# One transformer layer with a routed feed-forward on one core: where the patch embedding of the coming block stands in a six-stage software pipeline

## Chip, cores and metric

The kernel runs on one core of one Trainium2 chip, in one launch, all in float32. The metric is the device time of that launch in microseconds, the median of several runs.

## What is computed

32 images are cut into 36 patches of 768 numbers, embedded into 256 dimensions, and given a class token and position rows: 32 x 37 = 1184 tokens. One attention and one mixture-of-experts feed-forward follow, both on normalised input and both added to it:

```python
h = tok(x, W, b, pos_embd)                        # (32, 37, 256), class token in front
h = h + attn(layernorm(h))                        # q, k = rope(silu(x Wq)), rope(silu(x Wk)); 16 heads of 16
                                                  # out = (tril(q k^T)) v, no softmax
                                                  # out * sigmoid(x Wg1 Wg2), layernorm, @ Wo
h = h + moe(layernorm(h))                         # 32 experts of 4 groups, top 2 groups, top 6 experts;
                                                  # one shared expert; 1 of 16 anchor experts by the top expert
```

## The kernel before

**Tiles and blocks.** A tile (`TILES`) is three images, 111 tokens; there are eleven, the last with two images. Two tiles make a block (`BLOCKS`); there are six, block 5 holding the last tile alone, 74 tokens.

**Two halves of the program.** In the front half the blocks go through embedding, attention and routing. For each block the DVE (VectorE) works out, in `choose` and `place`, which row of a DRAM table `rows_d` each token takes in each of its seven lists (six experts and an anchor), and GpSimd writes the token's normalised row there by an indirect DMA (`scatter`, L385, one instruction L389 for a tile and choice, 77 in all). In the second half 112 list tiles of 128 rows are taken from `rows_d`, put through their expert's two matmuls, and added into `sums_d` by one indirect DMA each, again on GpSimd (`add_rows`, L404, instruction L409). At the end four copies of the sums are read back and added to `h` (L1217, L415).

**What orders the work.** Every engine has its own instruction list, written out by hand, and semaphores between them. The front half is a software pipeline: `stage(j)` (L289) names for j = -1 to 6 the block `coming` = j+1 (embedded in this stage), `ahead` = j (projected to q, k, v and gate), `mid` = j-1 (energies and attention, output projection) and `last` = j-2 (routed and ranked). The loops over j stand at L622 for TensorE (PE), L818 for ScalarE (ACT) and L1104 for the DVE. "Stage j" below means this j, and "mask of stage j" the DVE's first instruction of `mask_energy` in it.

**One stage on PE** (L622 to L668), for j = 2 to 4: `embed(coming, 0)`; `energies` of mid's first tile; `stay_busy(2)` (two matmuls whose result nobody reads, into B3, L517); `second_transposes(last)`; `stay_busy(1)`; `energies` of the second tile, in which each strip waits for the DVE to have masked the same strip of the first tile (L508); `attend` tile one, `route(last)`, `attend` tile two; `normed_transposes(ahead)`; `out_project(mid)`; `embed(coming, 1)`; `rank(last)`; `project(ahead)` (q and k, then v); `rotate`, `gate_inner`, `gate`. `embed` multiplies six chunks of the patches by the weights into bank B0, and its `pe.wait_ge(h_emb, b)` waits until the DVE has taken the block before out of B0. Every float32 matmul is two passes in the records, so an embedding of one tile is "x12".

**The first stages are different.** Stage -1 embeds block 0 and sends nine `stay_busy` matmuls behind it. Block 1's first tile is embedded at the end of stage 0 and its second in stage 1, between the energies. Stage 1 also folds the second layer norm's weights into the output projection: ACT scales `w_o` (`widen`, L732), PE multiplies (`fold`, L436), ACT copies a bias (`fold_bias`, L742), the DVE finishes (`fold`, L1084), and `embed` of block 2 waits for that (L427).

**One stage on the DVE** (L1104 to L1134), for j = 2 to 5: `mask_energy` of both tiles (L1036); `apply_gate(mid)` (L1046), which waits for both `attend`; `choose(last)`; `attended(mid)` (L1053 to L1068); `place(last)`, whose last instruction `slot` (L990) lets GpSimd go on with the block; `embedded(coming)` (L995: adds the position rows into `h`, L998, and takes the moments); `rope(ahead)` (L1019 to L1029), in which `add_bias` (L1007) stands; `norms()` (L916), one pass of inverse square roots for `last`'s coming second norm and for `coming`'s first. In stage 1 `embedded(1)` and its `norms` stand between the two masks, with the DVE's `fold` behind them.

**ACT** (L818 to L837) does `second_norm`, `second_copy`, `first_norm`, `scores`, `normed_copy`, `squares`, `qkv_copies`, `split_heads` (after the DVE's rope, releases the energies), `gate_tanh`.

**SyncE** issues the loads in one queue (L298 to L340): half of block 0's chunks, small constants, `w_qkv` and other constants (semaphore `consts`), patches of block 1, the weights of `rest`, patches of blocks 2 to 5, then the filling of `rows_d` and the experts' weights.

Of the kernel before, what the change touches and what calls it, by code (L numbers as in the profile page):

```python
# [78 lines left out]
def build(nc, pt, wt, posr, brow, wqkv, wo, wg1, wg2, lnwb, gwt, gbias, sgu, sd, wx,  # L79
          ident_c, cmask_c, turn_c, parity_c, cs_c, before_c, small_c, out):  # L80
    with ExitStack() as ctx:
# [216 lines left out]
        def _(sp):  # L298
# [6 lines left out]
            sp.dma_start(w_qkv[:, :, :], wqkv).then_inc(ld["consts"], 16)  # L305
            sp.dma_start(w_g1[:, :, :], wg1).then_inc(ld["consts"], 16)
            for dst, src in ((turn, turn_c), (w_g2, wg2), (parity, parity_c)):
                sp.dma_start(dst[:, :], src).then_inc(ld["consts"], 16)
            sp.dma_start(cossin[:, :, :], cs_c).then_inc(ld["consts"], 16)
# [5 lines left out]
            load_patches(1)  # L315
            for dst, src in ((w_o, wo), (ln_wb, lnwb), (w_route, gwt), (w_sgu, sgu)):
                sp.dma_start(dst[:, :, :], src).then_inc(ld["rest"], 16)
# [101 lines left out]
        def _(pe):  # L419
            def embed(b, i):  # L420
                t, at = BLOCKS[b][i], i * TT
                if b:
                    pe.wait_ge(ld[f"patch{b}"], 16)
                if i == 0 and b:
# [3 lines left out]
                for c in range(PC):  # L428
# [4 lines left out]
                if i == len(BLOCKS[b]) - 1:  # L433
                    m.then_inc(emb_ps, 1)
# [24 lines left out]
            def project(b):  # L459
                n = SIZES[b]  # L460
                pe.wait_ge(xnT_ok, b + 1)
                for half in range(2):
# [5 lines left out]
                    m.then_inc(qk_ps, 1)  # L468
                for t in BLOCKS[b]:
# [152 lines left out]
            for j in range(-1, NB + 1):  # L622
                coming, ahead, mid, last = stage(j)
                tiles = BLOCKS[mid] if mid is not None else []
                if coming is not None and j not in (0, 1):
                    embed(coming, 0)
                if j == -1:
                    embed(coming, 1)
                    stay_busy(9)
                if j == 0:  # L630
                    pe.wait_ge(ld["consts"], 16 * 8)
                if mid is not None:
                    energies(mid, tiles[0])
                if j == 1:
                    embed(ahead, 1)
                if last is not None and coming is not None:
                    stay_busy(2)
                if last is not None:
                    second_transposes(last)
                if last is not None and coming is not None:  # L640
                    stay_busy(1)
                for t in tiles[1:]:
                    energies(mid, t)
                if j == 1:
                    fold()
                if mid is not None:
                    attend(mid, tiles[0])
                if last is not None:
# [3 lines left out]
                if ahead is not None:  # L652
                    normed_transposes(ahead)
                if j == 1:
                    embed(coming, 0)
# [647 lines left out]
```

## Time and profile before

| | us |
|---|---|
| runs before: median (lowest, highest) of 3 | 471.47 (469.03, 471.80) |
| the profiled execution: its own time | 472.09 |
| its span, first to last instruction | 470.2 |
| GpSimd busy in it | 291.5 |
| PE busy, DVE busy, ACT busy | 369.0, 260.5, 202.1 |

The profile is one execution. Busy times of different engines overlap; a busy PE is not a PE at its peak. "Granted clock" is the share of full speed that TensorE's clock had (1.00 is 2.4 GHz, 0.50 is 1.2 GHz). The end of a matmul is modelled, so where the clock changes, what waits for it is the better witness.

### The profile page before, as it was taken

Reading aid. Unit: us, or ns where it says so; the run is one execution under the profiler, and the core shown is the slowest. Engines: PE = TensorE matmul, PEld = TensorE weight load, DVE = VectorE, ACT = ScalarE, POOL = GpSimd, SP = SyncE. Lnnn points to the kernel's source line nnn. Section 1 sums busy time; section 2 is a strip of 40 time slices with the busy share of each in tenths; the row PEclk is TensorE's granted clock in tenths of the full one; section 3 lists DMA queues with packets and bytes.
Section 4 is the critical chain, followed back from the end, with each engine's and each line's share of the span. In section 5 each row is a group of like instructions: output and inputs, shape, how many; then the busy total and the mean of one; then the engine's idle time right before and its main releaser. Section 6 shows DMA issues by size and latency. Waiting matters only on the chain.

```text
span 470.2 us, 10193 instructions
## 1 busy us (share of the span) xinstructions
PE 369.0 (78%) x2492; PEld 303.7 (65%) x2493; DVE 260.5 (55%) x1088; ACT 202.1 (43%) x581; POOL 291.5 (62%) x205
## 2 busy tenths in 40 slices
PE   6897999889987977367788799998999889998000
PEld 4666868568675865246566577887878787886000
DVE  0346668969588686674355445444454444444135
ACT  1132152341525222201266567677676767676000
POOL 3000000685848838886688888888888888888432
PEclk9998999979979565589599999999999999999655
DMA  8999998232329723893589998999989999997795
GB/s 237 314 338 316 428 366 316 49 84 54 81 67 360 164 56 79 265 321 101 135 149 154 158 157 150 158 160 151 156 146 163 153 151 160 158 153 102 159 265 166
DMA packets 67599, 85.81 MB, mean 182 GB/s; under 512 B 16984, under 2 KB 61446, under 8 KB 67318
## 3 DMA queue, kind: packets, MB, share of 16 engines
q1 hardware_dynamic: 37030, 59.82, 41.1%
q0 software_dynamic: 29680, 24.95, 36.0%
q10 hardware_dynamic: 864, 0.73, 0.5%
q8 instruction: 12, 0.20, 0.2%
q14 instruction: 13, 0.11, 0.1%
HBM read 45.86 MB, written 39.47 MB: 181 GB/s over the span
## 4 chain that ended last, share of the span: by engine, by line
PE 25%; DMA 19%; issue 16%; DVE 13%; POOL 13%; ACT 8%; ACTq 3%; SPq 1%; POOLq 0%; DVEq 0%
DMA sums_d<-e_sb,tok 13%; POOL rows_d L389 7%; PE B L431 6%; POOL sums_d L409 5%; PE B L466 3%; ACT UPW L852 3%; ACTq L276 2%; PE B L700 2%; DMA W<-sums_d 2%; PE B L529 2%; DMA e_sb<-rows_d 2%; ACT e_sb L875 2%; PE B L509 2%; DVE e_sb L1036 2%; PE B L712 2%
## 5 line engine op out<-in xcount | busy, mean ns | idle before, releaser
L409 POOL DMA_INDIRECT sums_d<-e_sb,tok x112 | 174.1, 1555 | 36.3 <-issue 24.6
L389 POOL DMA_INDIRECT rows_d<-xrow,slot x77 | 105.9, 1375 | 120.3 <-issue 103.9
L700 PEld LDWEIGHTS B<-e_sb,UPW 128*128 128x128 f32 x796 | 107.0, 195 | 10.3 <-issue 3.9
L700 PE MATMUL B<-e_sb,UPW 128*128 128x128 f32 x796 | 110.3, 280 | 0.0
L712 PE MATMUL B<-W,e_sb 128*128 x224 | 75.1, 417 | 21.4 <-issue 11.2
L1208 DVE TENSOR_TENSOR e_sb<-e_sb,B 128x128 f32<-128x128 f32 (+1 forms) x112 | 32.3, 288 | 83.9 <-ACT e_sb L863 58.9
L852 ACT COPY UPW<-W 128x512 f32 (+1 forms) x112 | 63.0, 562 | 0.7 <-issue 0.6
L712 PEld LDWEIGHTS B<-W,e_sb 128*128 128x128 f32 x224 | 34.2, 192 | 36.4 <-issue 35.4
L875 ACT ACTIVATE e_sb<-B,wcol 128x256 f32<-128x256 f32 x112 | 53.1, 474 | 0.0
L1192 DVE COPY e_sb<-B 128x256 f32<-128x256 f32 x112 | 46.9, 419 | 5.3 <-PE B L688 3.7
L688 PE MATMUL B<-ident,e_sb 128*128 128x128 f32 x224 | 44.7, 283 | 6.1 <-DMA e_sb<-rows_d 5.7
L874 ACT COPY tok<-tok_of 128x1 int32 (+1 forms) x112 | 21.5, 192 | 60.4 <-DMA sums_d<-e_sb,tok 36.1
L431 PE MATMUL B<-W 128*111 128x256 f32 (+1 forms) x132 | 35.8, 425 | 4.6 <-DMA W<-in_pt 4.6
L863 ACT ACTIVATE e_sb<-B 128x128 f32<-128x128 f32 (+1 forms) x112 | 30.8, 275 | 16.4 <-PE B L700 9.3
L688 PEld LDWEIGHTS B<-ident,e_sb 128*128 128x128 f32 x224 | 28.1, 145 | 8.3 <-DMA e_sb<-rows_d 4.5
L431 PEld LDWEIGHTS B<-W 128*111 128x111 f32 (+1 forms) x132 | 24.8, 196 | 12.7 <-DMA W<-in_pt 5.2
L1194 DVE TENSOR_TENSOR wcol<-e_sb,fresh (+1 forms) x112 | 17.8, 159 | 23.0 <-issue 18.1
L1036 DVE TENSOR_TENSOR e_sb<-B,causal 111x444 f32<-111x444 f32 (+1 forms) x44 | 23.6, 597 | 11.9 <-PE B L509 11.9
L767 ACT ACTIVATE W<-B 128x444 f32<-128x444 f32 (+1 forms) x12 | 6.0, 501 | 47.8 <-PE B L466 47.8
L1217 DVE TENSOR_TENSOR h<-h,W 112x256 f32<-112x256 f32 (+3 forms) x15 | 12.7, 867 | 19.3 <-DMA W<-sums_d 11.3
L466 PE MATMUL B<-W 128*128 128x222 f32 (+1 forms) x96 | 22.1, 396 | 0.6 <-ACT W L761 0.6
L466 PEld LDWEIGHTS B<-W 128*128 128x128 f32 x96 | 20.2, 234 | 1.3 <-ACT W L761 0.8
(167 smaller groups left out, 457.4 us busy)
## 6 DMA issues: line engine op xcount, KB each, us to landing
e_sb<-rows_d SPq DMA_DIRECT2D x112, 152.5 KB
rows_d<-padrow SPq DMA_DIRECT2D x1, 7320.0 KB, 34.5
W<-in_wx SPq DMA_DIRECT2D x1, 7027.0 KB, 50.6
sums_d<-padrow SPq DMA_DIRECT2D x4, 1408.0 KB, 22.5
W<-in_wx SPq DMA_DIRECT2D x1, 4576.0 KB
W<-in_wx SPq DMA_DIRECT2D x9, 478.5 KB
W<-in_pt SPq DMA_DIRECT2D x4, 666.0 KB, 8.7
sums_d<-e_sb,tok POOLq DMA_INDIRECT x112
```

The costliest lines, as they stand in the source:

```text
L389: pool.indirect_dma_start(rows_d, bass.IndirectOffsetOnAxis(ap=slot[0:n, t, j:j + 1], axis=0), xrow[0:n, t, :], None).then_inc(done, 16)
L409: pool.indirect_dma_start(sums_d[c], bass.IndirectOffsetOnAxis(ap=tok[:, c:c + 1], axis=0), Y[:, c, :], None, compute_op=ALU.add).then_inc ...
L431: m = pe.matmul(B[0][0:TILES[t], i * D:(i + 1) * D], patch_view(b)[:, c, at:at + TILES[t]], w_patch[:, c, :], start=c == 0, stop=c == PC - 1)
L466: m = pe.matmul(B[4 + half][:, c * BT:c * BT + n], w_qkv[:, k, lo:lo + P], xnT[:, k, 0:n], start=k == 0, stop=k == KC - 1)
L688: m = pe.transpose(B[u % 2][:, k * P:(k + 1) * P], G[:, u % 4, k * P:(k + 1) * P], ident[:, :])
L700: mm = pe.matmul(B[2 + u % 2][:, m * P:(m + 1) * P], UPW[:, u % 2, at:at + P], GT[:, u % 2, k, :], start=k == 0, stop=k == KC - 1)
L712: pe.matmul(B[6 + u % 2][:, 0:D], H[:, u % 2, :], W[:, bass.ds(e, size)][:, at:at + D], start=True, stop=True).then_inc(D_ps, 1)
L852: act.copy(UPW[:, u % 2, 0:n], weights[:, 0:n]).then_inc(upw_ok, 1)
L875: act.activation(Y[:, u % 4, :], B[6 + u % 2][:, 0:D], ACT.Copy, scale=wcol[:, bass.ds(i, 1)]).then_inc(Y_ok, 1)
L1036: dve.tensor_tensor(energy[0:n, i, 4 * r:4 * r + 4, 0:n], B[4 + r][0:n, 0:4 * n].rearrange("p (h t) -> p h t", h=4), causal[0:n, 0:n].unsq ...
L1192: dve.tensor_copy(GT[:, v % 2, :, :].rearrange("p k s -> p (k s)"), B[v % 2][:, 0:D]).then_inc(gt_ok, 1)
L1208: dve.tensor_tensor(H[0:n, u % 2, :], S[0:n, u % 2, :], ups, ALU.mult).then_inc(H_ok, 1)
```

## The change

- SyncE: the patches of block 1 are loaded ahead of `w_qkv` instead of behind `cossin`.
- Stage -1 on PE: three `stay_busy` matmuls instead of nine, and behind them the whole embedding of block 1. The DVE takes it out (`embedded(1)`, `norms`) in stage 0 ahead of `rope(0)`.
- The fold (`widen`, both `fold`, `fold_bias`) moves from stage 1 to the end of stage 0.
- `embed` gets a range of chunks. In stages 2 and 3 the second tile of the coming block is embedded in two halves of three chunks, one between the two energies and one behind the second; in stage 1 that place takes block 2's first tile, and its second stays behind the output projection. The three `stay_busy` matmuls of stages 2 to 4 go.
- `normed_transposes(ahead)` stands between the two `attend` in stage 1; elsewhere it stays behind both.
- `project` is split: q and k (`project_heads`) come right behind the output projection, then `rank(last)`, then v (`project_values`).
- DVE: `embedded(coming)` moves from behind `place` to between the masks and `apply_gate` (stages 2 to 4; in stage 1 it stays ahead of `rope`). `add_bias` moves out of `rope` to behind `norms`. `norms` waits for `xn_ok` of the block ahead.

The diff, cut to its lines and those next to them, indentation shortened:

```diff
@@ -302,17 +302,17 @@
...
         sp.dma_start(dst[:, :], src).then_inc(ld["consts"], 16)
+
+    def load_patches(b):
+        lo = PC * FIRST[b]
+        sp.dma_start(patches[:, lo:lo + PC * SIZES[b]], pt[:, lo:lo + PC * SIZES[b]]).then_inc(ld[f"patch{b}"], 16)
+
+    load_patches(1)
     sp.dma_start(w_qkv[:, :, :], wqkv).then_inc(ld["consts"], 16)
...
     sp.dma_start(cossin[:, :, :], cs_c).then_inc(ld["consts"], 16)
-
-    def load_patches(b):
-        lo = PC * FIRST[b]
-        sp.dma_start(patches[:, lo:lo + PC * SIZES[b]], pt[:, lo:lo + PC * SIZES[b]]).then_inc(ld[f"patch{b}"], 16)
-
-    load_patches(1)
     for dst, src in ((w_o, wo), (ln_wb, lnwb), (w_route, gwt), (w_sgu, sgu)):
@@ -417,20 +417,20 @@
...
 def _(pe):
-    def embed(b, i):
+    def embed(b, i, lo=0, hi=PC):
         t, at = BLOCKS[b][i], i * TT
-        if b:
+        if b and lo == 0:
             pe.wait_ge(ld[f"patch{b}"], 16)
-        if i == 0 and b:
+        if i == 0 and b and lo == 0:
             pe.wait_ge(h_emb, b)
...
                 pe.wait_ge(fold_ok, 1)
-        for c in range(PC):
+        for c in range(lo, hi):
             if b == 0 and i == 0:
...
                           w_patch[:, c, :], start=c == 0, stop=c == PC - 1)
-        if i == len(BLOCKS[b]) - 1:
+        if i == len(BLOCKS[b]) - 1 and hi == PC:
             m.then_inc(emb_ps, 1)
@@ -456,7 +456,7 @@
...

-    def project(b):
+    def project_heads(b):
         n = SIZES[b]
@@ -466,6 +466,8 @@
...
             m.then_inc(qk_ps, 1)
+
+    def project_values(b):
         for t in BLOCKS[b]:
@@ -622,50 +624,52 @@
...
         tiles = BLOCKS[mid] if mid is not None else []
-        if coming is not None and j not in (0, 1):
-            embed(coming, 0)
+        two = coming is not None and len(BLOCKS[coming]) > 1
         if j == -1:
-            embed(coming, 1)
-            stay_busy(9)
+            embed(0, 0)
+            embed(0, 1)
+            stay_busy(3)
+            embed(1, 0)
+            embed(1, 1)
         if j == 0:
             pe.wait_ge(ld["consts"], 16 * 8)
+        if coming is not None and j > 1:
+            embed(coming, 0)
         if mid is not None:
             energies(mid, tiles[0])
-        if j == 1:
-            embed(ahead, 1)
-        if last is not None and coming is not None:
-            stay_busy(2)
+        if two and j >= 1:
+            embed(coming, min(j - 1, 1), 0, PC // 2)
+        for t in tiles[1:]:
+            energies(mid, t)
+        if two and j >= 1:
+            embed(coming, min(j - 1, 1), PC // 2, PC)
         if last is not None:
             second_transposes(last)
-        if last is not None and coming is not None:
-            stay_busy(1)
-        for t in tiles[1:]:
-            energies(mid, t)
-        if j == 1:
-            fold()
         if mid is not None:
             attend(mid, tiles[0])
+        if j == 1:
+            normed_transposes(ahead)
         if last is not None:
...
             attend(mid, t)
-        if ahead is not None:
+        if ahead is not None and j != 1:
             normed_transposes(ahead)
-        if j == 1:
-            embed(coming, 0)
         if mid is not None:
             out_project(mid)
-        if coming is not None and len(BLOCKS[coming]) > 1 and j > 0:
+        if j == 1:
             embed(coming, 1)
+        if ahead is not None:
+            project_heads(ahead)
         if last is not None:
...
         if ahead is not None:
-            project(ahead)
+            project_values(ahead)
             rotate(ahead)
...
         if j == 0:
-            embed(coming, 0)
+            fold()
     second_transposes(NB - 1)
@@ -817,9 +821,6 @@
...
         _, ahead, mid, last = stage(j)
-        if j == 1:
-            widen()
-            fold_bias()
         if last is not None:
@@ -833,8 +834,12 @@
...
             qkv_copies(ahead)
+            if j == 0:
+                widen()
             split_heads(ahead)
             gate_tanh(ahead)
+        if j == 0:
+            fold_bias()
     second_norm(NB - 1)
@@ -913,8 +918,10 @@
...

-    def norms():
-
+    def norms(ahead):
+
+        if ahead is not None:
+            dve.wait_ge(xn_ok, BLOCKS[ahead][-1] + 1)
         step(dve.scalar_tensor_tensor(nwt[:, 0, 1:3, :], mv[:, 1:3, :, 1], EPS,
@@ -1017,8 +1024,6 @@
...
         step(dve.tensor_tensor(r, q, cossin[:, 0, :].unsqueeze(1).unsqueeze(1).to_broadcast(shape), ALU.mult))
-        if b:
-            add_bias(b)
         for half in range(2):
@@ -1103,17 +1108,17 @@
...
         coming, ahead, mid, last = stage(j)
+        if j <= 0:
+            embedded(coming)
+            norms(ahead)
         if j == 1:
             dve.wait_ge(ld["rest"], 16 * 8)
-            mask_energy(mid, BLOCKS[mid][0])
-            embedded(ahead)
-            norms()
-            mask_energy(mid, BLOCKS[mid][1])
-            fold()
+        for t in BLOCKS[mid] if mid is not None else []:
+            mask_energy(mid, t)
+        if j == 1:
             add_bias(mid)
-        else:
-            for t in BLOCKS[mid] if mid is not None else []:
-                mask_energy(mid, t)
+        if coming is not None and j > 1:
+            embedded(coming)
         if mid is not None:
@@ -1122,16 +1127,19 @@
...
             place(last)
-        if ahead == 0:
+        if j == 1:
+            embedded(coming)
+        if j == 0:
             dve.wait_ge(ld["consts"], 16 * 8)
             step(dve.tensor_scalar(base[:, :], base0, 1.0, None, ALU.add))
+        if ahead is not None:
             rope(ahead)
-        if coming is not None and j != 0:
-            embedded(coming)
-        if ahead is not None and ahead > 0:
-            rope(ahead)
-        if j != 0:
-            norms()
+        if j == 0:
+            fold()
+        if j > 0:
+            norms(ahead)
+        if ahead is not None and j > 0:
+            add_bias(ahead)
     choose(NB - 1)
...
```

## Rows read from the trace of the kernel before

**Rows 1.** Groups of GpSimd instructions: count, busy us, mean ns, idle us before them

```profile
L409 POOL DMA_INDIRECT sums_d<-e_sb,tok x112 | 174.1, 1555 | 36.3 <-issue 24.6 <-ACT e_sb L875 11.7
L389 POOL DMA_INDIRECT rows_d<-xrow,slot x77 | 105.9, 1375 | 120.3 <-issue 103.9 <-DVE slot L990 16.4
```

**Rows 2.** GpSimd's timeline: start us, duration us, instruction, idle time and its releaser

```profile
84.29 1.55 POOL L389 DMA_INDIRECT rows_d<-xrow,slot  x1 [79.58 <-issue]
...
111.62 1.35 POOL L389 DMA_INDIRECT rows_d<-xrow,slot  x1 [4.18 <-DVE slot L990]
...
141.24 1.35 POOL L389 DMA_INDIRECT rows_d<-xrow,slot  x1 [5.84 <-DVE slot L990]
...
170.81 1.48 POOL L389 DMA_INDIRECT rows_d<-xrow,slot  x1 [6.38 <-DVE slot L990]
...
212.57 1.36 POOL L389 DMA_INDIRECT rows_d<-xrow,slot  x1 [0.30 <-issue]
...
231.24 1.62 POOL L409 DMA_INDIRECT sums_d<-e_sb,tok  x1 [0.35 <-issue]
```

**Rows 3.** The DVE's timeline in stages 1 to 6, columns as in rows 2

```profile
32.71 2.20 DVE L1036 TENSOR_TENSOR e_sb<-B,causal 111x444 f32<-111x444 f32 x4 [4.36 <-PE B L509]
...
43.46 0.62 DVE L1046 SCALAR_TENSOR_TENSOR W<-W,B 128x444 f32<-128x444 f32 x1 [0.51 <-PE B L529]
...
64.81 2.20 DVE L1036 TENSOR_TENSOR e_sb<-B,causal 111x444 f32<-111x444 f32 x4 [1.90 <-PE B L509]
67.74 2.20 DVE L1036 TENSOR_TENSOR e_sb<-B,causal 111x444 f32<-111x444 f32 x4 [0.73 <-PE B L509]
71.04 0.62 DVE L1046 SCALAR_TENSOR_TENSOR W<-W,B 128x444 f32<-128x444 f32 x1 [1.10 <-PE B L529]
...
83.20 0.69 DVE L998 TENSOR_TENSOR h<-B,W 111x512 f32<-111x512 f32 x1
...
85.00 1.08 DVE L1019 TENSOR_TENSOR W<-W,cossin 128x888 f32<-128x888 f32 x1
...
91.45 2.19 DVE L1036 TENSOR_TENSOR e_sb<-B,causal 111x444 f32<-111x444 f32 x4
...
121.80 2.20 DVE L1036 TENSOR_TENSOR e_sb<-B,causal 111x444 f32<-111x444 f32 x4 [1.86 <-PE B L509]
...
148.93 2.20 DVE L1036 TENSOR_TENSOR e_sb<-B,causal 111x444 f32<-111x444 f32 x4
...
157.97 0.62 DVE L1046 SCALAR_TENSOR_TENSOR W<-W,B 128x444 f32<-128x444 f32 x1 [3.46 <-PE B L529]
...
175.25 1.57 DVE L1036 TENSOR_TENSOR e_sb<-B,causal 74x296 f32<-74x296 f32 x4
```

**Rows 4.** PE's timeline

```profile
13.21 4.05 PE L517 MATMUL B<-W 128*128 128x256 f32 x18
...
18.88 0.57 PE L456 MATMUL B<-ident,W 111*128 111x111 f32 x4 [1.63 <-ACT W L749]
...
47.26 1.03 PE L543 MATMUL B<-W 128*111 128x257 f32 x4
...
49.71 2.83 PE L431 MATMUL B<-W 128*111 128x256 f32 x12
...
90.36 1.02 PE L509 MATMUL B<-W 32*111 32x222 f32 x16 [0.91 <-ACT W L786]
...
104.77 3.75 PE L431 MATMUL B<-W 128*111 128x256 f32 x12
```

**Rows 5.** Two windows: length, busy PE, PEld, DVE, ACT, POOL, granted clock, DMA share, GB/s

```profile
99.90:106.70 6.80, 6.80 (x21) 5.37 (x22) 5.97 (x43) 1.77 (x2) 5.58 (x5) 0.50 0.39 94
...
151.00:171.20 20.20, 19.90 (x139) 16.52 (x134) 14.00 (x70) 5.28 (x12) 11.38 (x10) 0.50 0.59 152
```

**Rows 6.** The DMA issue at 8.42 us: count, size, us to landing

```profile
W<-in_pt SPq DMA_DIRECT2D x1, 666.0 KB, 8.1
```

**Rows 7.** ACT's timeline

```profile
29.93 0.90 ACT L737 ACTIVATE W<-W,ln_wb 128x256 f32<-128x256 f32 x2
```

## Prediction

> **What bounds the kernel now.** I begin with the groups of GpSimd's instructions [rows 1]. There are two: 77 scatters of 1.375 us and 112 additions of 1.555 us. Each is followed by some 0.30 us in which the queue waits for nothing shown, so a scatter costs 1.65 us and an addition 1.86 us. GpSimd's timeline [rows 2] then gives the frame. It starts at 84.29 us and from there it never has more than a few microseconds of rest. The reader is to see the three gaps, 4.18, 5.84 and 6.38 us, each ended by the DVE's `slot`: GpSimd has written a block's 14 tile-choices (14 x 1.65 = 23.2 us) and waits for the next block's places. From 170.81 on there is no such wait up to 231.24, where the additions begin 0.35 us behind the last scatter; 112 x 1.86 = 208 us later they are done, and some 31 us of reading back, adding and storing close the span of 470.2 us. So the end is the start of the fourth block's scatters plus 299.4 us, as long as nothing else in the front half is later than GpSimd. It nearly is: SyncE takes list rows only when the last anchor scatter (issued 212.57) has landed, and the shared expert on PE and DVE ends at about that time. A gain thus needs both: places for block 3 earlier, and the front half's computing earlier by as much.
>
> The DVE's timeline [rows 3] gives the stages. First masks of stages 1 to 6 stand at 32.71, 64.81, 91.45, 121.80, 148.93 and 175.25: stages of 32.1, 26.6, 30.4, 27.1 and 26.3 us, against GpSimd's 23.2. Which engine makes them so long is read from the idle time ahead of the rows. In stage 2 the DVE idles before both masks (1.90 and 0.73) and before the gate (1.10), and from 71.04 to 91.45 it works without a break: 20.4 us. PE's timeline [rows 4] has the other case, the first energies of stage 3 at 90.36, waiting 0.91 for ACT and so for the DVE's rope. So a stage is a piece M to A (mask to gate) in which PE and DVE wait for each other, and a piece A to M in which the DVE alone decides, unless PE is late with its embeddings. It was late in stage 3: the output projection and the embedding ran at half clock (3.75 against 2.83 us [rows 4]; granted clock 0.50 from 99.9 to 106.7 [rows 5]), PE reached the energies late and the DVE idled 1.86 before 121.80 [rows 3].
>
> **The front, stages -1 to 1.** Six of 18 passes of `stay_busy` remain: 4.05/3 = 1.35, PE free at 14.56 [rows 4]. Block 1's patches are issued some 2.8 us earlier, at 5.59; with the 8.1 us of [rows 6] they land at 13.7. Left where they were they would land at 16.5. The constants now behind them were all issued before 8.42 and, at that same delay, are there by 16.5 to 17; PE wants them at 20. Cost nothing. Two embeddings at 2.83 [rows 4], slightly overlapping, end at 20.2. The first transposes stood at 18.88, so all of stage 0 slips by 1.3. `widen` (two of its four activations 0.90 [rows 7], so at most 1.8) now stands ahead of `split_heads` on ACT, and the fold on PE (8 passes at 2.83/12, 1.9) ahead of the energies; behind the fold wait the energies alone, and the DVE's fold runs while PE does them. Ahead of those energies stood an embedding of 2.8. Energies and mask: + 1.3 - 2.8 + 1.9 + 0 to 1.2 of waiting for `widen`; I take +0.7 for the last, since about half of it lies under the gate matmuls. M1 is 32.71 + 1.1 = 33.8.
>
> M to A in stage 1 was 43.46 - 32.71 = 10.75; a whole embedding, a normalisation and the fold lay in it. New: the first mask and the wait for the second energies, 67.74 - 64.81 = 2.93 as in stage 2; then 3.30 (71.04 - 67.74), plus PE's second half embedding of 1.4 pushed ahead of the attention, less the 0.4 or so by which attention then waits less for the mask. The transposes between the attends replace a routing. So 7.2, A1 = 41.0 instead of 43.46. Output projection (49.71 - 47.26 = 2.45) after 0.7 for the gate: the second embedding starts at 44.15 instead of 49.71. From there to M2 PE's order is the same work, except that the embedding goes before q and k in both; PE had 15.1 us to 64.81. M2 = 59.25, **5.6 us earlier**. The DVE, freed of nothing in this stretch, ends attended, embedded, rope, norms and bias at about 58, so PE decides.
>
> **Stages 2 to 4, M to A.** Stages 2 and 3: 6.23 of before (71.04 - 64.81), plus half an embedding 1.4, plus the second transposes, now behind the second energies, 0.57 (as four matmuls in [rows 4]), less 0.2 to 0.4 of mask waiting. I take 8.0. The first half embedding lies in the wait for the mask. Bounds for the two halves together: 0, if all is cover, and 2 x 1.9 at half clock (half of 3.75); taken 1.4. The DVE fills this wait with `embedded`, 85.00 - 83.20 = 1.80 [rows 3]. Stage 4 has one tile coming and no halves: 6.6. The dropped `stay_busy` lay in the same waits and gives nothing back.
>
> **A to M.** The DVE's 20.41 less 1.80 is 18.6; `add_bias` only changes its place. PE's 2.8 of embedding is out of it, q and k start right behind the output projection, and the embedding that stays ahead of the energies is done about 1 us before rope: no stage is PE's any more. The wait put into `norms` costs nothing: `xn_ok` comes from ACT before PE's transposes, 15 us earlier. `rank` behind q and k costs nothing at full clock: `place` ends 12.2 us after A (83.20 - 71.04) and takes them some 1.3 before that, and PE has them by 0.7 + 2.45 + 3.8 + 1.9 = 8.9 at most (16 and 8 passes at 2.83/12).
>
> So M3 = 59.25 + 8.0 + 18.6 = 85.85, A3 93.85, M4 = 112.45, A4 = 119.05, M5 = 137.65. Stage 5 as before, 157.97 - 148.93 = 9.04 to A5 = 146.7, 17.28 more to M6, with 0.7 for ranks behind q and k at half clock (0.50 from 151.0 to 171.2 [rows 5]): 164.7. Against before: 5.6, 5.6, 9.35, 11.3, 10.6 us earlier.
>
> **GpSimd.** First start was A2 + 13.25, the fourth A5 + 12.84 [rows 2, 3]. New: 67.25 + 13.25 = 80.5; 93.85 + 12.84 = 106.7; 131.9; 146.7 + 12.84 + 0.7 = 160.2, each later than 23.2 us behind the one before, so gaps of 3.0, 2.0 and 5.1 remain. The fourth is 10.6 earlier than 170.81, computing is earlier by the same, and the additions run in the same rhythm: span 470.2 - 10.6 = 459.6. The profiled execution took 472.09, 1.9 beyond its span, and stands 0.6 above the median of the runs, 471.47. So 461.5 in its own terms, 460.9 in the median's; **I say 461.**
>
> **A rule against the change.** The dropped matmuls kept TensorE occupied. In the rows the clock is 0.50 for 6.8 us behind a light stretch in stage 3 and for 20.2 us in stage 5, where no embedding stands among the small matmuls [rows 5]. The Trainium skill, "TensorE: Matmul & The Clock Gate", in its Part 1 on the clock gate, says that the throttled state is the default and activity lifts it; in its section on a second failure mode it has small pauses between groups of matmuls enough to make the clock oscillate. By that rule the stages without dummies would run at half clock and the kernel would take the time of the slow rival below; by the rows, real embeddings of full width now stand where the dummies stood, except in stage 4.
>
> **Rivals.**
> 1. *Only the front gains.* PE's lateness in stage 3 was the clock's, and some other wait (ACT's table and copies between transposes and scores, late rank) holds stages 3 and 4 at 30.4 and 27.1 us. For: the DVE, which I call the bound, is merely close to it. Against: it works 20.4 us unbroken in stage 2. Then everything is 5.6 earlier: 465.9.
> 2. *Clock lost in stages 2 to 4; slower.* If the clock falls between masks and gate, half embeddings and attention double: M to A grows from 8.0 by the 2.8 that stage 5 shows over stage 2 (9.04 - 6.23) and by 1.4 more for the second half, and the ranks, now behind q and k, come 2 us late for `place`: 6.2 us a stage. Three stages are 18.6 - 10.6 = 8 us slower: 479. It decides from the second such stage on.
> 3. *GpSimd alone.* Stages come down to 23.2, no gaps: fourth start 80.5 + 69.6 = 150.1, 20.7 earlier: 451. Against: the DVE has 18.6 + 4.4 of masks + 1.8 + waits, over 25.
> 4. *It doesn't do what it says*: block 1's patches are late, and stage 0 slips by more than stage 1 wins. Price 16.5 - 14.56 = 2: 463.
>
> **Chances and range.** Forecast 0.55 (457 to 464.5); rival 1 0.20; rival 2 0.09 (with one stage cold, 467; with two, 473); rival 3 0.06; rival 4 0.10. The range 454 to 469 takes in rivals 1 and 4, one cold stage, and below, stage 5 at full clock (2.4 us less from M to A, no rank delay) with the half embeddings wholly covered (up to 2 x 1.4); it leaves out the rest of 2 and part of 3. About 1%, 4.7 us, is what a measurement can tell from no change. Faster by more (under 466.8): 0.79. Within: 0.14. Slower: 0.07.
>
> **What would show it.** First energies-mask of stages 2 to 6 near 59, 86, 112, 138, 165; GpSimd's first and fourth block at 80.5 and 160, three gaps of 2 to 5 us; PE idle about 1 us before the energies of stages 3 and 4; M to A near 8, no DVE wait from A to M. Wrong if: masks of stage 4 or 5 less than 7 us earlier (rival 1), granted clock 0.50 before the gates of stages 2 to 4 (rival 2), the additions starting later than right behind the last scatter (the front's computing is then the bound).

## Result and the profile after

The changed kernel takes 465.8 us (median of 20 runs) against 470.04 (20 runs) of the kernel before: ratio 0.9907, 95% interval 0.9883 to 0.9931. A second group of runs gave 466.64 against 468.95, ratio 0.9956 (0.9930 to 0.9981). So the change gains 2 to 4 us, and the forecast of 461 (10.5 gained) was too good by some 5. The profiled execution has a span of 463.5 and took 465.33; that of before took 472.09, 2 us above its own kernel's median of 20, so 6.7 us between the two traces stand for 4.2 between the medians.

The page of the changed kernel: granted clock and GpSimd in 40 slices (tenths), and GpSimd's two groups with count, busy us, mean ns and idle time before them.

```profile
span 463.5 us, 10136 instructions
...
POOL 3000000886858668886788888888888888888433
PEclk9999999999596555588599999999999999999555
...
L409 POOL DMA_INDIRECT sums_d<-e_sb,tok x112 | 174.1, 1555 | 35.2 <-issue 26.8
L389 POOL DMA_INDIRECT rows_d<-xrow,slot x77 | 107.3, 1394 | 113.2 <-issue 101.0
```

The groups are those of [rows 1]: 1.56 and 1.39 us, the same rhythm, so the gain is in when the work starts. The clock's digits are near full speed up to slice 10, then 5 in slice 11 (115.9 to 127.5 us), 9 in slice 12, and 5 or 6 in slices 13 to 17. Next GpSimd's timeline, to be laid beside [rows 2].

```profile
80.87 1.55 POOL L389 DMA_INDIRECT rows_d<-xrow,slot  x1 [76.15 <-issue]
...
107.06 2.04 POOL L389 DMA_INDIRECT rows_d<-xrow,slot  x1 [2.78 <-DVE slot L997]
...
135.65 2.04 POOL L389 DMA_INDIRECT rows_d<-xrow,slot  x1 [4.36 <-DVE slot L997]
...
164.89 1.35 POOL L389 DMA_INDIRECT rows_d<-xrow,slot  x1 [4.99 <-DVE slot L997]
...
206.33 1.36 POOL L389 DMA_INDIRECT rows_d<-xrow,slot  x1 [0.30 <-issue]
...
213.93 1.35 POOL L389 DMA_INDIRECT rows_d<-xrow,slot  x1 [2.94 <-issue]
...
225.53 1.62 POOL L409 DMA_INDIRECT sums_d<-e_sb,tok  x1 [0.30 <-issue]
```

First start 80.87 (before 84.29), fourth 164.89 (170.81), additions from 225.53 (231.24). The three gaps are 2.78, 4.36 and 4.99; the forecast had 3.0, 2.0 and 5.1, so the second is the one that it missed. The last anchor scatter is issued at 206.33 (before 212.57, the fifth row of [rows 2]). Two scatters behind it GpSimd pauses for 2.94 us with nothing shown that it waits for; the kernel before has such a pause too, 2.37 us ahead of 219.61. The fourth start is 5.92 earlier, the first addition 5.71, and 1.0 more is won in the additions and their end. The DVE's masks and gates, to be laid beside [rows 3]:

```profile
59.66 2.20 DVE L1041 TENSOR_TENSOR e_sb<-B,causal 111x444 f32<-111x444 f32 x4 [1.29 <-PE B L511]
...
67.61 0.62 DVE L1051 SCALAR_TENSOR_TENSOR W<-W,B 128x444 f32<-128x444 f32 x1 [1.15 <-issue]
...
86.05 2.19 DVE L1041 TENSOR_TENSOR e_sb<-B,causal 111x444 f32<-111x444 f32 x4
...
94.58 0.62 DVE L1051 SCALAR_TENSOR_TENSOR W<-W,B 128x444 f32<-128x444 f32 x1 [1.73 <-issue]
...
113.07 2.19 DVE L1041 TENSOR_TENSOR e_sb<-B,causal 111x444 f32<-111x444 f32 x4
116.45 2.20 DVE L1041 TENSOR_TENSOR e_sb<-B,causal 111x444 f32<-111x444 f32 x4 [1.18 <-PE B L511]
...
123.10 0.62 DVE L1051 SCALAR_TENSOR_TENSOR W<-W,B 128x444 f32<-128x444 f32 x1 [3.45 <-PE B L531]
...
141.66 2.19 DVE L1041 TENSOR_TENSOR e_sb<-B,causal 111x444 f32<-111x444 f32 x4
...
151.63 0.62 DVE L1051 SCALAR_TENSOR_TENSOR W<-W,B 128x444 f32<-128x444 f32 x1 [4.40 <-PE B L531]
...
169.69 1.57 DVE L1041 TENSOR_TENSOR e_sb<-B,causal 74x296 f32<-74x296 f32 x4
```

| | before | forecast | measured |
|---|---|---|---|
| first mask, stage 2 | 64.81 | 59.25 | 59.66 |
| first mask, stage 3 | 91.45 | 85.85 | 86.05 |
| first mask, stage 4 | 121.80 | 112.45 | 113.07 |
| mask to gate, stages 2, 3 | 6.23, 7.71 | 8.0, 8.0 | 7.95, 8.53 |
| mask to gate, stage 4 | 7.02 | 6.6 | **10.03** |
| first mask, stage 5 | 148.93 | 137.65 | 141.66 |
| mask to gate, stage 5 | 9.04 | 9.04 | 9.97 |
| first mask, stage 6 | 175.25 | 164.7 | 169.69 |
| fourth block's scatters | 170.81 | 160.2 | 164.89 |

Up to the mask of stage 4 every step is within 0.7 us. Of the 4.7 us missing at the fourth block, 3.4 arise in one place, between mask and gate of stage 4, where the DVE idles 3.45 us for PE. Another 0.6 us was there at the mask of stage 4, and 0.9 comes from mask to gate of stage 5. The windows of the same kernel (length, busy PE, PEld, DVE, ACT, POOL, granted clock, DMA share, GB/s) and PE's timeline of stage 4 say why.

```profile
86.00:113.00 27.00, 24.26 (x201) 18.29 (x199) 22.61 (x94) 10.28 (x22) 20.26 (x15) 1.00 0.31 73
...
114.40:127.60 13.20, 13.20 (x106) 10.41 (x106) 8.08 (x38) 5.37 (x9) 10.76 (x9) 0.50 0.73 260
...
141.70:199.60 57.90, 43.39 (x261) 35.55 (x262) 39.98 (x207) 14.00 (x31) 43.31 (x32) 0.50 0.48 140
```

```profile
107.68 2.82 PE L431 MATMUL B<-W 128*74 128x256 f32 x12
111.49 1.02 PE L511 MATMUL B<-W 32*111 32x222 f32 x16 [0.98 <-ACT W L790]
113.83 3.30 PE L511 MATMUL B<-W 32*111 32x222 f32 x16 [1.32 <-DVE e_sb L1041]
...
117.99 1.71 PE L531 MATMUL B<-e_sb,W 111*32 111x111 f32 x32
...
128.28 3.25 PE L466 MATMUL B<-W 128*128 128x222 f32 x16
```

PE embeds block 5's only tile, waits 0.98 for ACT, does the first energies, waits 1.32 for the mask, and in the second energies the clock goes to 0.50: 3.30 us for them where the first took 1.02, 1.71 for an attention that takes 0.97 at full clock (91.10 in stage 3 of this trace). It stays there for all of the 13.2 us of the second window with PE busy all the time, is back at 127.8 us in the output projection's second tile, so that q and k (128.28) run at full clock, and is lost again in stage 5 for 57.9 us.

### The profile page after: what moved, and what is told of

It reads as the page before. It is cut to its first block, busy times and chain, and to the rows that moved or that the text cites. A ratio compares the mean times of both kernels' runs of the same rounds, so it can differ in the third digit from the quotient of the medians.

```text
span 463.5 us, 10136 instructions
## 1 busy us (share of the span) xinstructions
PE 366.1 (79%) x2462; PEld 301.3 (65%) x2463; DVE 260.3 (56%) x1088; ACT 201.3 (43%) x581; POOL 293.7 (63%) x205
## 4 chain that ended last, share of the span: by engine, by line
issue 20%; PE 19%; DMA 19%; DVE 14%; POOL 12%; ACT 8%; ACTq 5%; SPq 2%; DVEq 0%; POOLq 0%
DMA sums_d<-e_sb,tok 12%; POOL rows_d L389 7%; PE B L431 4%; POOL sums_d L409 4%; ACT UPW L857 4%; PE B L511 3%; ACTq L276 3%; PE B L531 2%; PE B L466 2%; DMA W<-in_pt 2%; DMA W<-sums_d 2%; ACT e_sb L880 2%; DVE h L1225 2%; DMA rows_d<-xrow,slot 1%; PE B L545 1%
## 5 line engine op out<-in xcount | busy, mean ns | idle before, releaser
L409 POOL DMA_INDIRECT sums_d<-e_sb,tok x112 | 174.1, 1555 | 35.2 <-issue 26.8
L389 POOL DMA_INDIRECT rows_d<-xrow,slot x77 | 107.3, 1394 | 113.2 <-issue 101.0
L704 PEld LDWEIGHTS B<-e_sb,UPW 128*128 128x128 f32 x796 | 107.0, 195 | 10.5 <-issue 4.9
L431 PE MATMUL B<-W 128*111 128x256 f32 (+1 forms) x132 | 33.7, 404 | 6.1 <-DMA W<-in_pt 5.9
L868 ACT ACTIVATE e_sb<-B 128x128 f32<-128x128 f32 (+1 forms) x112 | 30.8, 275 | 17.7 <-PE B L704 10.4
L431 PEld LDWEIGHTS B<-W 128*111 128x111 f32 (+1 forms) x132 | 22.8, 181 | 14.7 <-DMA W<-in_pt 6.8
L511 PE MATMUL B<-W 32*111 32x222 f32 (+1 forms) x176 | 19.6, 424 | 6.7 <-ACT W L790 4.0
L511 PEld LDWEIGHTS B<-W 32*111 32x111 f32 (+1 forms) x176 | 12.8, 194 | 12.5 <-ACT W L790 5.2
L466 PE MATMUL B<-W 128*128 128x222 f32 (+1 forms) x96 | 19.8, 366 | 0.6 <-ACT W L765 0.6
```

Of the source, the lines that this page charges most:

```text
L389: pool.indirect_dma_start(rows_d, bass.IndirectOffsetOnAxis(ap=slot[0:n, t, j:j + 1], axis=0), xrow[0:n, t, :], None).then_inc(done, 16)
L409: pool.indirect_dma_start(sums_d[c], bass.IndirectOffsetOnAxis(ap=tok[:, c:c + 1], axis=0), Y[:, c, :], None, compute_op=ALU.add).then_inc ...
L431: m = pe.matmul(B[0][0:TILES[t], i * D:(i + 1) * D], patch_view(b)[:, c, at:at + TILES[t]], w_patch[:, c, :], start=c == 0, stop=c == PC - 1)
L511: m = pe.matmul(B[4 + r][0:n, 2 * k * n:2 * (k + 1) * n], qk[strip, KC + k, at:at + n], q_two[strip, :, k, at:at + n], start=True, stop=True)
L704: mm = pe.matmul(B[2 + u % 2][:, m * P:(m + 1) * P], UPW[:, u % 2, at:at + P], GT[:, u % 2, k, :], start=k == 0, stop=k == KC - 1)
L868: act.activation(S[0:n, u % 2, :], B[2 + u % 2][0:n, 0:P], ACT.Silu).then_inc(silu_ok, 1)
```

## The experiments

**The changed kernel again.**

> The changed kernel itself, for a second trace and as the yardstick of this group. Clock theory: the granted clock falls to 0.50 between the two energies of stage 4 again, mask to gate takes about 10.0 us there against the 6.6 forecast, and the time is 4 to 5 us below the kernel before. Rival (the first trace was one chance execution): stage 4 at full clock, mask to gate near 6.6, and more than 6 us gained.

Measured: 466.64, ratio 0.9956 (0.9930 to 0.9981). In its trace stage 4 has half clock from 114 to 124, 10.03 from mask (112.75) to gate (122.78); stage 5's mask at 141.56. The time is 2.3 us under that of before, where 4 to 5 were expected. The loss in stage 4 came in both traces, so it was no chance of the first one.

**The kernel before again.**

> The kernel before, for a second trace. Chance theory (the half-clock stretch from 99.9 to 106.7 us in stage 3 of the first trace is a matter of the execution, not of the order of the work): no such stretch or one elsewhere, stage 3 near 26.6 us instead of 30.4, and a time near 469 instead of 472.1. Rival (the order of stage 3 causes it): half clock in stage 3 again and a stage of 30 us.

```profile
94.00:122.60 28.60, 26.14 (x209) 20.16 (x209) 22.81 (x94) 10.93 (x23) 20.46 (x15) 0.94 0.30 70
...
104.00:107.00 3.00, 3.00 (x11) 2.40 (x10) 2.69 (x19) 0.17 (x1) 2.39 (x3) 0.50 0.36 90
```

Measured: 470.35 us in one run. Stage 3 took 28.65 us (93.99 to 122.64), between the two expectations: half clock again at the same place of the stage, but for 3.4 us (103.8 to 107.2) and not for 6.8 as in [rows 5]. So the length of the stretch is the execution's, and 1.7 of the 30.4 us of stage 3 in the trace that I forecast from were bad luck. There was good luck as well: the first mask of stage 2 stands at 67.34 here, 2.5 later than in [rows 3], behind half clock from 18.4 to 25.2 us, which the first trace does not have.

**Stage 4 filled.**

```diff
+                if j == 4:
+                    stay_busy(3)
                 for t in tiles[1:]:
                     energies(mid, t)
```

> The changed kernel with three matmuls of no use put back between the two energies of stage 4, where no half embedding stands. Clock theory: granted clock 1.00 there, mask to gate 6.6 to 7.1 instead of 10.0, mask of stage 5 near 138.3 instead of 141.7, fourth block's scatters 3 us earlier, and the time 3 us below the changed kernel's. Rival (the DVE's new order or the late ranks hold the stage): mask to gate stays near 10 and the time is the same or up to 1 us longer.

PE, then the DVE, then two windows of this kernel:

```profile
112.86 1.02 PE L511 MATMUL B<-W 32*111 32x222 f32 x16 [1.53 <-ACT W L792]
113.81 1.56 PE L519 MATMUL B<-W 128*128 128x256 f32 x6
115.30 2.38 PE L511 MATMUL B<-W 32*111 32x222 f32 x16
```

```profile
114.44 2.19 DVE L1043 TENSOR_TENSOR e_sb<-B,causal 111x444 f32<-111x444 f32 x4
117.36 2.20 DVE L1043 TENSOR_TENSOR e_sb<-B,causal 111x444 f32<-111x444 f32 x4 [0.73 <-PE B L511]
...
121.05 0.62 DVE L1053 SCALAR_TENSOR_TENSOR W<-W,B 128x444 f32<-128x444 f32 x1 [0.49 <-PE B L531]
```

```profile
114.40:121.00 6.60, 6.60 (x98) 4.80 (x97) 5.36 (x12) 3.37 (x6) 5.38 (x5) 1.00 0.37 83
121.00:137.00 16.00, 12.36 (x70) 10.22 (x69) 14.44 (x69) 5.09 (x14) 12.65 (x10) 1.00 0.93 336
```

Measured: 463.33, ratio 0.9883 (0.9847 to 0.9918), 3.3 below the changed kernel of the same group. Mask to gate is 6.61, the forecast's 6.6, at clock 1.00: 1.4 us of matmuls that nobody reads, laid into a wait, give back 3.4. In its trace the stages stand 1.4 us later (114.44 against 113.07 at this mask) behind half clock from 31.6 to 35.0 us, so the mask of stage 5 stands at 139.86, not at 138.3.

**Stages 4 and 5 filled**, twice. The operands are those of `w_qkv`, since `w_patch` is being overwritten by then.

```diff
+            def fill(n):
+                for _ in range(n):
+                    pe.matmul(B[3][:, 0:D], w_qkv[:, 0, 0:P], w_qkv[:, 0, 0:D], start=True, stop=True)
...
+                if j == 5:
+                    pe.wait_ge(h2_ok, BLOCKS[mid][0])
+                    fill(4)
                 if mid is not None:
                     energies(mid, tiles[0])
                 if two and j >= 1:
                     embed(coming, min(j - 1, 1), 0, PC // 2)
+                if j in (4, 5):
+                    fill(3)
                 for t in tiles[1:]:
                     energies(mid, t)
```

> The changed kernel with unused matmuls in stage 4 (three between the energies, as before) and in stage 5 (four ahead of the energies, three between them). Clock theory: full clock until the gate of stage 5, mask to gate there 6.6 instead of 10.0, the mask of stage 6 3 us earlier than with stage 4 filled alone, GpSimd's gap before block 3 gone, and the time 2 to 3 us below it. Rival (stage 5's small matmuls lose the clock whatever stands among them): mask to gate stays 9 to 10, same time as with stage 4 alone.

> The kernel with stages 4 and 5 filled, again, as the yardstick of this group: ratio to before between 0.978 and 0.986, the time near 461.

```profile
112.81 2.19 DVE L1051 TENSOR_TENSOR e_sb<-B,causal 111x444 f32<-111x444 f32 x4
...
120.33 0.62 DVE L1061 SCALAR_TENSOR_TENSOR W<-W,B 128x444 f32<-128x444 f32 x1 [1.40 <-PE B L536]
...
138.78 2.19 DVE L1051 TENSOR_TENSOR e_sb<-B,causal 111x444 f32<-111x444 f32 x4
...
145.52 0.62 DVE L1061 SCALAR_TENSOR_TENSOR W<-W,B 128x444 f32<-128x444 f32 x1 [1.61 <-PE B L536]
...
161.87 1.57 DVE L1051 TENSOR_TENSOR e_sb<-B,causal 74x296 f32<-74x296 f32 x4
```

```profile
158.38 1.35 POOL L389 DMA_INDIRECT rows_d<-xrow,slot  x1 [1.45 <-DVE slot L1007]
...
219.11 1.62 POOL L409 DMA_INDIRECT sums_d<-e_sb,tok  x1 [0.30 <-issue]
223.91 1.59 POOL L409 DMA_INDIRECT sums_d<-e_sb,tok  x1 [3.18 <-ACT e_sb L890]
```

Measured: 461.61, ratio 0.9809 (0.9766 to 0.9852), and 459.51, ratio 0.9785 (0.9748 to 0.9821). Stage 4's 7.52 from mask to gate is 6.61 in the second trace. From mask to gate stage 5 takes 6.74 (second trace 6.55) instead of 9.97, and the mask of stage 6 comes at 161.87 instead of 169.69. GpSimd's gap before block 3 is 1.45, not gone. The fourth block is 6.5 us earlier than in the changed kernel, the span 4.5: the second list tile's addition waits 3.18 us for its rows, so the first list tiles, and no longer the scatters alone, set the end there. Which of the seven unused matmuls of stage 5 are needed was not tried. This is the time that I had forecast for the change alone.

**More filling.** Against the kernel with stages 4 and 5 filled (the operands now from `w_sgu`):

```diff
-                if j == 5:
+                if j in (5, 6):
                     pe.wait_ge(h2_ok, BLOCKS[mid][0])
-                    fill(4)
+                    fill(4 if j == 5 else 10)
...
-                if j in (4, 5):
+                if j in (4, 5, 6):
                     fill(3)
...
             pe.wait_ge(hs_ok, NB)
+            fill(6, 4)
```

> As fill45, with unused matmuls in stage 6 too (ten ahead of its energies, three behind them) and six ahead of the first list tile. Clock theory: full clock in stage 6's attention and routing, about 1.5 us less from its mask to its choice, and 1 to 3 us less at the first list tiles, where GpSimd waited 3.18 us for the second tile; time 1 to 3 us below fill45. Rival (behind stage 5 the DVE and the scatters alone decide): the same time within 1 us.

Measured: 458.53, ratio 0.9792 (0.9754 to 0.9830). The clock was 1.00 from 140 to 169 us, but the median is only 1.0 us under that of stages 4 and 5 filled in the same group (459.51), its ratio is not below theirs (0.9785), and the intervals cover each other: the two are not told apart.

**Front alone.** Stage -1, the fold and `norms` as changed, from stage 2 on the order as before, except that `add_bias` stays behind `norms`; in stage 1 the embedding stays around the output projection. PE's order against the kernel before:

```diff
                 if j == -1:
-                    embed(coming, 1)
-                    stay_busy(9)
+                    embed(0, 0)
+                    embed(0, 1)
+                    stay_busy(3)
+                    embed(1, 0)
+                    embed(1, 1)
...
-                if j == 1:
-                    embed(ahead, 1)
...
-                if j == 1:
-                    fold()
...
                 if j == 0:
-                    embed(coming, 0)
+                    fold()
```

> The kernel before with the front part of the change alone: block 1 embedded in stage -1, patches and fold earlier; stages 2 to 6 in the old order, with their unused matmuls. My theory (front gains 5.2 by the mask of stage 2, reordered stages then win 3.5 in stage 3 and lose it again in stages 4 and 5): mask of stage 2 at 59.7, time 4 to 6 us below before, the same as the changed kernel within 1.5 us. Rival (the reordered stages carry the gain): time within 2 us of before.

Measured: 466.86, ratio 0.9966 (0.9939 to 0.9994); as fast as the whole change in the same group. The mask of stage 2 came at 63.16, not at 59.7: a half-clock stretch at 37 to 44 us in stage 1, where no half embedding stands between the energies. Stages 2 to 5 then took 26.5, 26.9, 26.3 and 25.5 us (the changed kernel 26.4, 27.0, 28.6 and 28.0), and the fourth block started at 164.81. So in the two traces the new order is 3.5 us ahead at stage 2 and loses that in stages 4 and 5; on balance it gives nothing measurable. Stages 2 and 3 are as long in the old order as in the new: stage 3 has no half-clock stretch here, and its 30.4 us of before are gone without any reordering of it.

**Before, without its nine unused matmuls.**

```diff
-                if last is not None and coming is not None:
-                    stay_busy(2)
                 if last is not None:
                     second_transposes(last)
-                if last is not None and coming is not None:
-                    stay_busy(1)
```

> The kernel before without its nine unused matmuls in stages 2 to 4 and nothing else changed. Clock theory: the granted clock falls between mask and gate of at least one of the three stages, mask to gate there 9 to 10 us instead of 6.2 to 7.7, and the time is 2 to 6 us longer than before. Rival (they did nothing): same time within 1 us.

The gate of stage 4 in the kernel before, 7.02 us behind its mask at 121.80:

```profile
128.82 0.62 DVE L1046 SCALAR_TENSOR_TENSOR W<-W,B 128x444 f32<-128x444 f32 x1 [1.88 <-PE B L529]
```

Measured: 470.77, ratio 1.0036 (1.0013 to 1.0060), 1.8 us longer than before in the same group, a little less than the 2 to 6 expected. In the trace mask to gate of stage 4 is 9.04 us (119.79 to 128.83) instead of 7.02, at a mean clock of 0.55. Stages 2 and 3 take 6.23 and 7.27 from mask to gate, no longer than before, so the loss shows in stage 4 alone. They had been doing something.

**Ranks ahead of q and k.**

```diff
-                if ahead is not None:
-                    project_heads(ahead)
                 if last is not None:
                     rank(last)
                 if ahead is not None:
+                    project_heads(ahead)
                     project_values(ahead)
```

> The changed kernel with the ranks ahead of q and k again. My forecast's term (ranks behind q and k cost nothing at full clock and 0.7 us at half clock in stage 5; q and k earlier gain nothing, since the DVE sets the pace): the same time within 1 us, and no wait of the DVE before the ranks' reading in stage 5. Rival (ranks first hold q and k back until the choice is made): the DVE waits at rope and the stages grow by 1 us or more.

PE behind the output projection of stage 2:

```profile
70.17 0.46 PE L548 MATMUL B<-ones,W 128*111 128x1 f32 x4
72.43 0.62 PE L581 MATMUL B<-chosen,before 111*111 111x48 f32 x4 [1.81 <-DVE chosen L971]
...
74.09 5.99 PE L466 MATMUL B<-W 128*128 128x222 f32 x16
```

Measured: 471.63, ratio 1.0011 (0.9981 to 1.0041): against 0.9907 and 0.9956 of the changed kernel this one place costs 2.6 to 4.9 us, about the whole gain. PE waits 1.81 for the choice, the ranks and then q and k run at half clock, 5.99 us instead of 3.25, PE comes late to the next energies, and stages 2 and 3 take 30.0 and 30.8 us.

**The same with that wait filled** by four unused matmuls into bank B0 (`fill` as above).

```diff
+                if last is not None and coming is not None:
+                    pe.wait_ge(h_emb, coming + 1)
+                    fill(4)
                 if last is not None:
                     rank(last)
```

> The ranks ahead of q and k, as in the run before, but with four unused matmuls (into a free bank) in the wait between output projection and ranks of stages 2 to 4. Clock theory (PE's 1.6 to 1.8 us of waiting for the choice loses the clock, and q and k then take 5.9 us instead of 3.1): q and k near 3.2 us, stages 2 and 3 back at 26.5 to 27.5 us instead of 30.0 and 30.8, time 4 to 6 us below ranks first unfilled. Rival (waiting for the choice itself is what costs): stages stay near 30 and the time near 471.

```profile
71.08 0.46 PE L553 MATMUL B<-ones,W 128*111 128x1 f32 x4
71.40 1.97 PE L524 MATMUL B<-W 128*128 128x256 f32 x8
73.35 0.59 PE L586 MATMUL B<-chosen,before 111*111 111x48 f32 x4
...
74.41 3.23 PE L466 MATMUL B<-W 128*128 128x222 f32 x16
```

Measured: 465.93, ratio 0.9940 (0.9911 to 0.9969), 0.7% or 3.3 us less by the two ratios, where 4 to 6 were expected. The ranks come no earlier: 1.81 us behind the end of the output projection (73.35 behind 71.54, unfilled 72.43 behind 70.63) and 13.10 us behind the mask of stage 2 in both traces. q and k take 3.23 us instead of 5.99, and the stages are 26.7 and 26.8 us. So it is not the wait that costs: the clock lost in it costs 3.3 (30.0 - 26.7) to 4.0 us a stage in these traces. They lie further apart than the kernels do (473.18 and 462.27, the latter the fastest of its 12 runs), so the price in the mean is the 3.3 us of the ratios.

**Embedding taken out late on the DVE**, behind `place`.

```diff
                 if j == 1:
                     add_bias(mid)
-                if coming is not None and j > 1:
-                    embedded(coming)
                 if mid is not None:
                     apply_gate(mid)
...
                 if last is not None:
                     place(last)
-                if j == 1:
+                if coming is not None and j > 0:
                     embedded(coming)
```

> The changed kernel with the DVE taking the coming block out of PSUM behind the placing again, as before the change. My forecast's term (between masks and gate the DVE idles anyway, so this work lies there for nothing): the DVE idles 3 us before the gates of stages 2 and 3 instead of 1.2 to 1.7, these stages grow by about 1.8 us each and the time by 3 to 4. Rival (it only moves the idle time): same time within 1 us.

```profile
60.70 2.20 DVE L1041 TENSOR_TENSOR e_sb<-B,causal 111x444 f32<-111x444 f32 x4 [1.29 <-PE B L511]
...
68.59 0.62 DVE L1051 SCALAR_TENSOR_TENSOR W<-W,B 128x444 f32<-128x444 f32 x1 [2.76 <-PE B L531]
```

Measured: 470.80, ratio 1.0008 (0.9986 to 1.0030); 2.4 to 4.7 us longer than the changed kernel by the ratios. The DVE idles 2.76 before the gate of stage 2 and 2.67 in stage 3, and the stages take 28.1 and 28.9 us, 1.7 and 1.9 more; stage 3 has 3.4 us of half clock in this trace (88.4 to 91.8) which the changed kernel does not have, so stage 2's 1.7 is the clean figure.

**The coming tile embedded whole** behind the second energies.

```diff
-                if two and j >= 1:
-                    embed(coming, min(j - 1, 1), 0, PC // 2)
                 for t in tiles[1:]:
                     energies(mid, t)
                 if two and j >= 1:
-                    embed(coming, min(j - 1, 1), PC // 2, PC)
+                    embed(coming, min(j - 1, 1))
```

> The changed kernel with the coming tile embedded whole behind the second energies instead of in two halves around them. My forecast's term (the first half lies in the wait for the mask): mask to gate grows by 1.4 us in stages 2 and 3, from 8.0 to 9.4, and by as much in stage 1, time 3 to 5 us longer than the changed kernel. Clock theory adds: the wait between the energies is then empty, and half clock may begin in stage 2 or 3 already; then 6 us or more. Rival (the halves are cosmetic): same time within 1 us.

```profile
94.17 3.31 PE L511 MATMUL B<-W 32*111 32x222 f32 x16 [1.33 <-DVE e_sb L1039]
97.41 4.72 PE L431 MATMUL B<-W 128*111 128x256 f32 x12
```

Measured: 476.11, ratio 1.0148 (1.0101 to 1.0195), 9 to 11 us longer than the changed kernel by the ratios: mask to gate 10.9 in stage 2 and 11.9 in stage 3. The clock goes at the empty wait between the energies or soon behind it (in stage 3 3.31 us for the second energies and 4.72 for an embedding of 2.8) in stages 1, 2 and 3, from 36.4, 67.1 and 94.4 us, as the clock theory's addition had it.

## Why the prediction was wrong

**What bounds the kernel: right.** GpSimd's rhythm and the start of the fourth block set the end; 5.9 us there became 6.7 in the span. The sum of the miss at the fourth block, 4.7 us: 0.6 up to the mask of stage 4, 3.4 and 0.9 from mask to gate of stages 4 and 5, and 0.3 less behind that. One reading was off: "From 170.81 on there is no such wait up to 231.24" passes over the pause of 2.37 us at 219.61. It is 2.94 us in the changed kernel, 0.6 more.

**The front: right.** Mask of stage 2 forecast 59.25, measured 59.66. It is nearly the whole of what the change gains: with it alone the time is 466.86, with all of the change 466.64. Block 1's patches held PE until 14.90 instead of 14.56, and the embeddings ended at 20.3.

**Mask to gate, the step that failed.** "Stage 4 has one tile coming and no halves: 6.6. The dropped `stay_busy` lay in the same waits and gives nothing back." The first sentence holds at full clock (6.61 with stage 4 filled). The second is the error: I priced the dropped matmuls by the PE time they take, and that is nothing, but what they kept was the clock. In stages 2 and 3 the half embeddings took over that duty, in stage 4 nothing did, and it cost 3.4 us there. The sign that I had set for rival 2, 0.50 ahead of a gate of stages 2 to 4, came in stage 4. The Trainium skill, "TensorE: Matmul & The Clock Gate", Part 1, has half speed as the default that activity lifts. The traces agree in stage 4: 0.50 from 114.4, and 1.00 there with three matmuls more. Stages 2 and 3, with embeddings where the unused matmuls stood, stayed at 1.00 up to there (86.0 to 113.0 in the windows). I had named stage 4 as the exception and then put no microsecond on it; rival 2 with one cold stage stood at 467, at 6.2 us a stage where 3.4 were measured.

**Rival 1's number, not its mechanism.** "Everything is 5.6 earlier: 465.9" is all but the measured 465.8, by luck. No other wait holds stages 3 and 4 at 30.4 and 27.1 us: stage 3 takes 27.0, the masks of stages 4 and 5 are 8.7 and 7.3 us earlier, above its limit of 7, and stage 4 filled takes 25.4 from mask to mask. Against the first trace of before the changed kernel is 8.7 us ahead at the mask of stage 4 and 5.6 at that of stage 6; what it loses between them it loses at half clock.

**Stage 5, mis-sized.** "Stage 5 as before", 27.0 us with the ranks; measured 28.0. With PE's work done earlier its wait ahead of the energies is 1.99 us instead of 0.79, half clock begins at 141.5, ahead of the second energies (138.1 in the second trace; before at 151.0, within them), and from mask to gate it takes 9.97. Freed of it (stages 4 and 5 filled) the stage takes 23.1. I took a stage that was already at half clock as a constant, when it was the largest thing left to gain.

**Ranks behind q and k: right in sum, wrong in reason.** I had them at nothing at full clock. That is so only because the edit keeps the clock full: with the embedding gone from between output projection and ranks, ranks first would have cost 3 to 5 us.

**The DVE's order: right.** 1.80 a stage forecast, 1.7 and 1.9 measured by taking it back. The halves' term was right as well (mask to gate of stage 2 7.95, forecast 8.0), and it cancels the DVE's: stage 2 takes 26.4 us against 26.6 before. What the halves do besides, keeping the clock, is worth more: whole behind the energies they cost 9 to 11 us.

**The base.** I gave stage 3's 30.4 us back in full, 3.75 of the 10.5 us, as the work of the new order. That gain was the half-clock stretch's: the second trace of before has 28.65 in their place, and front alone, in the old order and at full clock, 26.9 against the changed kernel's 27.0. Whether the new order shortens stage 4 when its clock is kept is not shown: stage 4 filled takes 25.4 us, front alone 26.3, but with half clock in it from 129 to 133 us. And 470.04, not 471.47, is the median of more runs, so another 1.4 us of the forecast gain were never there in the mean.

## What to carry to other kernels

Before taking an idle-looking matmul out, or moving real ones out of a gap, list for every stage what TensorE does in the stretch it shortens and look at the granted clock there; price the edit by the stretch at half clock, not by the matmuls' own time. If a wait of one to two microseconds among small matmuls cannot be removed, try matmuls in it, real ones if there are any and unused ones if not, and look at the clock again; here three of 128x128 by 256 columns gave back 3.3 us. A stage that stands at half clock already is a place to gain, not a constant.

## What the runs showed that I had not expected

- A busy PE row does not mean a full clock: PE was busy 13.2 of 13.2 us at 0.50 in stage 4, with energies, attention, routing, transposes and the first tile of the output projection. The clock was back at 127.8 us, in the second tile. In stage 5 the output projection, q, k and v ran at 0.50 from end to end, so none of these brings it back by itself; what does was not tried. The Trainium skill, "TensorE: Matmul & The Clock Gate", in its section on a second failure mode, speaks of pauses between groups of matmuls. The pauses of 0.98 and 1.32 us ahead of the second energies fit that; the 13.2 unbroken us at half clock behind them are not explained by it.
- The wait for the ranks was free and the clock lost in it was not: four unused matmuls in that wait left the ranks where they were, 13.10 us behind the mask, and the kernel took 0.7% less.
- The length of a half-clock stretch at the same place differs from execution to execution (6.8 and 3.4 us in stage 3 of the kernel before, none in the same order in front alone), and stretches that begin between 30 and 38 us come and go (31.6 with stage 4 filled, none in the changed kernel). Why the same program differs so is open.
